# A two-layer graph network on one core: the f32 adjacency enters through 64 casting transfers issued by GpSimd and is recoded in place, instead of through strips cast by ScalarE and VectorE

## The chip, the core and the metric

The kernel runs on one core of a Trainium2 chip. A core has TensorE (PE, matrix products), VectorE (DVE), ScalarE (ACT), GpSimd (POOL) and SyncE (SP), which run side by side, each through its own list of instructions in order, and wait for one another at semaphores. Sixteen DMA engines move data between the device's memory and SBUF, the on-chip memory of 128 partitions. The metric is the time of one execution on the device in microseconds (us); lower is better.

## What is computed

x has 4096 nodes of 256 features, adj is a 4096 x 4096 matrix of zeros and ones in f32. The reference, cut to what matters:

```python
deg = jnp.maximum((adj != 0).astype(jnp.float32).sum(-1), 1.0)
x = _layernorm(x + _L0_gnn_ref(x, adj, deg[..., None], L0_gnn_W, L0_gnn_b), axis=-1)
x = _layernorm(x + _L1_gnn_ref(x, adj, adj, ...), axis=-1)

def _L0_gnn_ref(x, adjacency, node_degree, W, b):
    a_norm = dinv * (adjacency + eye) * dinv          # dinv = rsqrt(node_degree)
    return relu((a_norm @ x + x) @ W + b)

def _L1_gnn_ref(x, adj_a, adj_b, W_sa, a_sa, W_gcnb, b_gcnb, Wa, ba, Wb, bb):
    attn_a = sigmoid(concat([adj_a @ x, x], 1) @ Wa.T + ba)
    attn_b = sigmoid(concat([adj_b @ x, x], 1) @ Wb.T + bb)
    h = x @ W_sa
    scores = s_left[:, None] + s_right[None, :]       # both from h and a_sa
    e = where(adj_a != 0, exp(-leaky_relu(scores, 0.01)), 0.0)
    x_a = (e / (sum(e, axis=1) + 1e-05)) @ h
    x_b = adj_b @ (x @ W_gcnb) + b_gcnb
    return sigmoid(attn_a * x_a + attn_b * x_b)
```

## The kernel before

The 4096 rows are 32 tiles of 128 (`T`); the adjacency's columns are 16 panels of 256 (`PW`), two panels are a quad of four tiles, and there are 8 quads (`NQ`). The work has three stages.

**First products (0 to about 60 us).** x comes in six pieces (`x_in`, cut at tiles 0, 2, 4, 8, 16, 24, 32). A loop over the 32 tiles lets PE transpose a tile of x (L1333) and multiply it by W0 to z (L1348). ACT copies the transposed tile and, for the first 12 tiles, z; DVE copies z from tile 12 on (`ZACT`, L804). z is split into a high half (ACT, L529) and a low half (DVE, L831) in f16, after a scale that needs the largest value of x: DVE reduces each piece (L798), POOL reduces across partitions (L422). From step 14 on PE adds, in each step, one block of 128 adjacency rows to the sums of the first four tiles (`pass0_rows`, L1365). Between these, DVE and PE work out a norm of the weights; POOL raises it to a power (L425) for which DVE waits in `weight_scale` (L869 on) at step 25.

**First network (to about 323 us).** For each tile n PE sums 32 blocks of the adjacency, as fp8 codes, times z's halves (`sum_rows`, L1365; 64 matmuls). DVE makes degree, residual and statistics, POOL the reciprocal root (L441, a power) and the next tile's z plus bias (L434), DVE normalises (L990). PE transposes the result (`t_step`), ACT and DVE split it into two halves (L548, L946), PE projects it by the second network's weights (`p_step`, L1400). ACT copies the projections; POOL forms sums of them (`g_sums`, L278 to L280), ACT and DVE split those too (`forms_hi` L582 to L584, `forms_lo` L921 to L926).

**Second network (to the end).** 16 panels, each read back from a scratch in device memory into `pan` (L354 for the first two, L387 in the loop). DVE forms differences of panel blocks (L940), PE the products (L1470), ACT exponentials (L624), DVE masks them by the panel's codes (L1099), and PE multiplies them by h (L1529).

**How the adjacency comes in.** SP loads strips of 2 row blocks x 512 columns of f32 (512 KB, `strip`, a ring of 6; 128 strips, L341). Even strips are cast by ACT (L509), odd ones by DVE (L791), both to one byte per entry, 8 for an edge (2^-6 in fp8) and 128 (minus zero) for none, into `codes`, which holds three quads (`SLOTS`). A strip's slot in the ring comes free when it is cast, a quad's slot in `codes` when its four tiles are summed (`acc_done`) and its codes have been written to the scratch (`codes_out`, L329). SP issues the small weights after the fifth strip (`WTS_AT`). Where in its list an engine casts is written out by hand: `cast(count)` calls stand between its other steps.

## Time and profile before

| what | value |
|---|---|
| median of 3 runs | 880.51 us (879.71 to 880.66) |
| span of the profiled execution, first to last instruction | 877.3 us |
| busy: PE, DVE, ACT, POOL | 856.7, 683.4, 571.2, 181.3 us |
| granted TensorE clock, mean | 0.996 of full speed |
| DMA queue of SP / of ACT | 120.87 MB / 8.38 MB |

The profile is of one execution. For that execution only the span is given; the time of a whole run holds a few microseconds more than the span. Busy times of engines lie beside one another; a line such as L341 is a line of the kernel before.

### The profile page before, as it was taken

How to read it: one execution, taken by the hardware profiler on the slowest of the kernel's cores; microseconds unless marked ns; L12 is line 12 of the kernel's file. 1: busy time of each engine (PE TensorE's matmuls, PEld its weight loads, DVE VectorE, ACT ScalarE, POOL GpSimd, SP SyncE). 2: the span in 40 equal slices, each digit the busy share in tenths (PEclk: the TensorE clock that was granted, in tenths of full speed). 3: DMA queues.
4: the chain of work that ended last, by engine and by line, in shares of the span. 5: the costliest groups of instructions: out<-in, count | busy, mean ns of one | idle time of the engine just before them, and what ended most of it. 6: DMA issues, size and time to landing. Idle time of an engine off the chain costs nothing.

```text
span 877.3 us, 20460 instructions
## 1 busy us (share of the span) xinstructions
PE 856.7 (98%) x7579; PEld 755.0 (86%) x7579; DVE 683.4 (78%) x1182; ACT 571.2 (65%) x1214; POOL 181.3 (21%) x181
## 2 busy tenths in 40 slices
PE   8899999999999998999999999999999999999997
PEld 7787888888888887887788888888888888888886
DVE  5787676766667567898988988988978978978863
ACT  5754555555555237988977976966966967867831
POOL 1001333323322321012022022032032032032021
PEclk9999999999999999999999999999999999999999
DMA  9989999998999424110220120120120220220001
GB/s 321 305 273 320 352 401 339 360 344 315 380 316 341 174 105 144 56 55 1 79 80 15 63 78 24 54 78 15 63 78 6 71 78 0 78 78 0 25 25 37
DMA packets 66617, 130.01 MB, mean 148 GB/s; under 512 B 5464, under 2 KB 29056, under 8 KB 62080
## 3 DMA queue, kind: packets, MB, share of 16 engines
q1 hardware_dynamic: 57632, 120.87, 39.2%
q10 hardware_dynamic: 8928, 8.38, 2.8%
q8 instruction: 36, 0.59, 0.3%
q14 instruction: 21, 0.17, 0.1%
HBM read 99.87 MB, written 29.36 MB: 147 GB/s over the span
## 4 chain that ended last, share of the span: by engine, by line
PE 76%; issue 11%; DVE 5%; ACT 3%; DMA 3%; POOL 1%; SPq 0%; POOLq 0%; ACTq 0%; DVEq 0%
PE ps L1529 31%; PE ps L1365 21%; PE ps L1470 19%; PE ps L1400 4%; ACT ec L624 2%; DVE ec L1099 1%; DMA xs<-in_x_dram 1%; ACT em L633 1%; DMA h_scratch<-hst 1%; PE ps L1385 1%; DVE em L1106 1%; DVE dd L940 0%; POOL zb L434 0%; DMA x1r<-x_scratch 0%; SPq L335 0%
## 5 line engine op out<-in xcount | busy, mean ns | idle before, releaser
L1529 PE MATMUL ps<-fb,em 128*128 128x257 f16 x3072 | 347.5, 273 | 0.8 <-DVE em L1106 0.8
L1529 PEld LDWEIGHTS ps<-fb,em 128*128 128x128 f16 x3072 | 300.5, 98 | 38.6 <-issue 1.3
L1365 PE MATMUL ps<-y,codes 128*128 128x257 f16 x2048 | 237.8, 273 | 0.4 <-DVE y L831 0.4
L1365 PEld LDWEIGHTS ps<-y,codes 128*128 128x128 fp8e4 x2048 | 200.2, 98 | 27.0 <-DVE y L831 0.8
L624 ACT ACTIVATE ec<-slb,nsb 128x256 f32<-128x256 f32 x512 | 211.3, 499 | 0.0
L1106 DVE SCALAR_TENSOR_TENSOR em<-ec,em 128x2048 f16<-128x2048 f32 x64 | 147.4, 2303 | 22.7 <-ACT em L633 22.7
L633 ACT ACTIVATE em<-ec 128x2048 f16<-128x2048 f32 x64 | 122.1, 1910 | 65.1 <-PE ps L1529 57.0
L1099 DVE SCALAR_TENSOR_TENSOR ec<-ec,pan 128x2048 f32<-128x2048 f32 x64 | 147.3, 2302 | 2.6 <-issue 1.8
L1470 PE MATMUL ps<-zz,dd 128*128 128x256 f16 x768 | 89.4, 273 | 1.5 <-DVE t L1128 1.3
L458 POOL TENSOR_TENSOR sc<-sc,sc 128x2 f32<-128x2 f32 x15 | 38.5, 2569 | 246.3 <-DVE sc L1208 246.3
L1470 PEld LDWEIGHTS ps<-zz,dd 128*128 128x128 fp8e4 x768 | 75.0, 98 | 10.7 <-issue 2.0
L509 ACT ACTIVATE codes<-strip 128x1024 uint8<-128x1024 f32 x64 | 65.5, 1049 | 19.5 <-DMA strip<-in_adj_dram 18.6
L452 POOL TENSOR_TENSOR w<-w,bgb 128x512 f32<-128x512 f32 x16 | 27.7, 1732 | 184.6 <-DVE w L1166 184.6
L1470 PE MATMUL ps<-fa,pan 128*128 128x260 f16 x512 | 61.7, 279 | 3.4 <-DVE s L1137 2.1
L940 DVE SCALAR_TENSOR_TENSOR dd<-pan 128x512 uint32<-128x512 uint32 (+2 forms) x85 | 64.1, 815 | 0.0
L1470 PEld LDWEIGHTS ps<-fa,pan 128*128 128x128 fp8e4 x512 | 50.7, 99 | 11.6 <-issue 2.3
L441 POOL TENSOR_TENSOR lnst<-lnst,sc 128x1 f32<-128x1 f32 x32 | 24.8, 774 | 173.0 <-DVE lnst L984 173.0
L1470 PE MATMUL ps<-fa,dd 128*128 128x260 f16 x512 | 59.6, 274 | 0.4 <-DVE m L1118 0.4
L791 DVE TENSOR_SCALAR codes<-strip 128x1024 uint8<-128x1024 f32 x64 | 49.6, 777 | 10.7 <-DMA strip<-in_adj_dram 10.7
L1470 PEld LDWEIGHTS ps<-fa,dd 128*128 128x128 fp8e4 x512 | 49.9, 98 | 7.6 <-issue 0.9
L548 ACT ACTIVATE x1t<-ps 128x256 f16<-128x256 f32 x32 | 12.3, 383 | 60.0 <-PE ps L1385 60.0
L669 ACT ACTIVATE ot<-sg,sc 128x256 f32<-128x256 f32 x30 | 16.4, 593 | 52.5 <-POOL sc L462 52.5
(154 smaller groups left out, 786.0 us busy)
## 6 DMA issues: line engine op xcount, KB each, us to landing
strip<-in_adj_dram SPq DMA_DIRECT2D x128, 512.0 KB, 7.5
a_scratch<-codes SPq DMA_DIRECT2D x16, 1024.0 KB, 10.3
pan<-a_scratch SPq DMA_DIRECT2D x16, 1024.0 KB, 4.9
x_scratch<-x ACTq DMA_DIRECT2D x32, 128.0 KB, 5.3
x1r<-x_scratch SPq DMA_DIRECT2D x16, 256.0 KB, 2.8
h_scratch<-hst ACTq DMA_DIRECT2D x30, 136.0 KB, 5.5
out_dram<-ot SPq DMA_DIRECT2D x15, 256.0 KB, 2.2
fb<-h_scratch SPq DMA_DIRECT2D x3, 1088.0 KB, 8.8
```

Of the source, the lines that this page charges most:

```text
L458: pool.tensor_tensor(sc1[:, RS2], sc1[:, VE2], sc[:, MH2], ALU.pow).then_inc(S["yrstd_ready"], 1)
L509: act.activation(codes_of(s), strip_of(s), ACT.Copy, scale=float(EDGE - NONE), bias=float(NONE)).then_inc(S["cast_act"], 1)
L624: e_ = act.activation(ec[:, c % ER, jj, :], slb[:, slot, :], ACT.Exp, scale=-(1 - SLOPE), bias=nsb[:, jb:jb + 1])
L633: act.activation(em[:, c, 0], ec[:, c % ER], ACT.Copy, scale=MU / EDGE_VAL).then_inc(S["ehigh_ready"], 1)
L791: dve.tensor_scalar(codes_of(s), strip_of(s), float(EDGE - NONE), float(NONE), ALU.mult, ALU.add).then_inc(S["cast_dve"], 1)
L940: return dve.scalar_tensor_tensor(out=o, in0=b, scalar=0x7f7f7f7f, in1=a, op0=ALU.bitwise_and, op1=ALU.bitwise_xor)
L1099: dve.scalar_tensor_tensor(out=ec[:, c % ER], in0=ec[:, c % ER], scalar=1.0, in1=pan[:, slot, c * CH:(c + 1) * CH, :].bitcast(F8), op0=ALU ...
L1106: dve.scalar_tensor_tensor(out=em[:, c, 1], in0=ec[:, c % ER], scalar=MU / EDGE_VAL, in1=em[:, c, 0], op0=ALU.mult, op1=ALU.subtract).then ...
L1365: mm = pe.matmul(ACC(n), codes[:, qq % SLOTS, h, jb, e * P:(e + 1) * P].bitcast(F8), y[:, jb, part, 0:YC], start=(jb == 0 and part == 0), ...
L1400: mm = pe.matmul(b, x1t[:, n % 2, x_part, k * P:(k + 1) * P], wps[:, k, w_part, c0:c1], start=(k == 0 and x_part + w_part == 0), stop=(k = ...
L1470: mm = pe.matmul(ps[:, bank, 0:2 * c], a.bitcast(F8), g, start=(p == 0), stop=(p == NP - 1))
L1529: mm = pe.matmul(PH(2 * m + e)[:, 0:HC], em[:, c, e_part, i, e * P:(e + 1) * P], fb[:, jb, h_part, 0:HC], start=(jb == 0 and e_part + h_pa ...
```

## The change

The strips, their ring and all casts go. POOL issues 64 transfers (`load_codes`), each of 4 row blocks x 512 columns: 1 MB of f32 is read, and the DMA engines write it as fp8 straight into a quad's slot of `codes`. There an edge is 0x38 and no edge 0x00; DVE recodes a chunk in place over 32-bit words (`code`): an exclusive or with 0x20 in each byte, then a shift left by two bits, which gives 0x60 (32.0) and 0x80 (minus zero). The constant `EDGE_VAL` goes from 2^-6 to 32 in all scales. DVE recodes at the places where it cast; ACT's casts at their places are gone. Each of the 24 chunks that fit into `codes` has its own semaphore. `codes` and the scratch now keep a quad's 512 columns of a row block together, so the quad's codes leave in one transfer of 2 MB, and a panel is read back as 256 bytes per row block and partition. SP loads the small weights right after x. PE, SP and ACT wait for DVE's recodes alone (`coded`). The first chunks are issued when the fifth piece of x has come (`x_in[4]`).

```diff
-SJ = 2
-GS = T // SJ
-NSTRIP = NQ * GS
-RING = 6
+CJ = 4
+GS = T // CJ
+NCHUNK = NQ * GS
...
-EDGE, NONE = 8, 128
-EDGE_VAL = 2.0 ** -6
+EDGE_VAL = 32.0
+ZERO_BIT, RAISE = 0x20202020, 2
...
-    codes = at("codes", [P, SLOTS, 2, T, PW], U8, O_C)
-    strip = at("strip", [P, RING, SJ, 2 * PW], F32, O_S)
+    codes = at("codes", [P, SLOTS, T, 2 * PW], U8, O_C)
...
-    a8d = nc.dram_tensor("a8_scratch", [NPAN, P, T, PW], U8)
+    a8d = nc.dram_tensor("a8_scratch", [NQ, P, T, 2 * PW], U8)
...
-            def codes_when_cast(qq):
-
-                for sem, n in zip(("cast_act", "cast_dve"), casts_until(qq * GS + GS - 1)):
-                    sp.wait_ge(S[sem], n)
-                for h in range(2):
-                    sp.dma_start(a8d[2 * qq + h], codes[:, qq % SLOTS, h]).then_inc(codes_out[qq % SLOTS], 16)
+            def codes_when_coded(qq):
+
+                sp.wait_ge(S["coded"], (qq + 1) * GS)
+                sp.dma_start(a8d[qq], codes[:, qq % SLOTS]).then_inc(codes_out[qq % SLOTS], 16)
...
-            for s in range(NSTRIP):
-                if s >= RING:
-                    sp.wait_ge(S["cast_act" if on_act(s - RING) else "cast_dve"],
-                               casts_until(s - RING)[0 if on_act(s - RING) else 1])
-                qq, g = s // GS, s % GS
-                sp.dma_start(strip[:, s % RING], adj_view[:, g * SJ:(g + 1) * SJ, qq * 2 * PW:(qq + 1) * 2 * PW]
-                             ).then_inc(strip_in[s % RING], 16)
-                if s == WTS_AT:
-                    load_weights()
-                if s >= RING and (s - RING) % GS == GS - 1:
-                    codes_when_cast((s - RING) // GS)
+            load_weights()
+            for qq in range(NQ - 1):
+                codes_when_coded(qq)
...
-                sp.dma_start(pan[:, m], a8d[m]).then_inc(panel_in[m], 16)
+                sp.dma_start(pan[:, m], a8d[0, :, :, m * PW:(m + 1) * PW]).then_inc(panel_in[m], 16)
...
-                sp.dma_start(pan[:, m], a8d[s + 2]).then_inc(panel_in[m], 16)
+                sp.dma_start(pan[:, m], a8d[bass.ds(qq, 1), :, :, m * PW:(m + 1) * PW].rearrange("q p t i -> p (q t) i")
+                             ).then_inc(panel_in[m], 16)
...
+            def load_codes(c0, c1):
+
+                for c in range(c0, c1):
+                    qq, g = c // GS, c % GS
+                    if qq >= SLOTS and g == 0:
+                        pool.wait_ge(S["acc_done"], PT * (qq - SLOTS + 1))
+                        pool.wait_ge(codes_out[qq % SLOTS], 16 * (qq // SLOTS))
+                    pool.dma_start(codes[:, qq % SLOTS, g * CJ:(g + 1) * CJ, :].bitcast(F8),
+                                   adj_view[:, g * CJ:(g + 1) * CJ, qq * 2 * PW:(qq + 1) * 2 * PW]
+                                   ).then_inc(codes_in[c % (SLOTS * GS)], 16)
+
             pool.wait_ge(S["const_ready"], 2)
             pool.wait_ge(S["wabs_ready"], 1)
             pool.partition_all_reduce(wabs[:, 1, :], wabs[:, 0, :], P, RADD).then_inc(S["wz_all"], 1)
+            pool.wait_ge(x_in[4], 16)
+            load_codes(0, 3)
             pool.wait_ge(S["xmax_part"], 1)
             pool.partition_all_reduce(sc[:, XALL], sc[:, XMX], P, RMAX).then_inc(S["xmax_all"], 1)
 
+            load_codes(3, SLOTS * GS)
             pool.wait_ge(S["wnorm_ready"], 1)
             pool.tensor_tensor(sc[:, WN], sc[:, WMX], sc[:, MH], ALU.pow).then_inc(S["alpha_pow"], 1)
...
                 if n + 2 < T:
                     z_with_bias(n + 2)
+                first = SLOTS * GS + (n - PT + 1) * 2
+                if SLOTS * GS <= first < NCHUNK:
+                    load_codes(first, first + 2)
                 if n == 3:
                     g_sums(pool, 0)
                 if n >= 4 and n % 2 == 0:
...
-        def cast_waits(eng, s):
-
-            qq = s // GS
-            eng.wait_ge(strip_in[s % RING], 16 * (s // RING + 1))
-            if qq >= SLOTS:
-                eng.wait_ge(S["acc_done"], PT * (qq - SLOTS + 1))
-                eng.wait_ge(codes_out[qq % SLOTS], 32 * (qq // SLOTS))
...
-            def cast(count):
-
-                for s in [next(todo) for _ in range(count)]:
-                    cast_waits(act, s)
-                    act.activation(codes_of(s), strip_of(s), ACT.Copy, scale=float(EDGE - NONE),
-                                   bias=float(NONE)).then_inc(S["cast_act"], 1)
-
...
-            for sem, n in zip(("cast_act", "cast_dve"), casts_until(NSTRIP - 1)):
-                act.wait_ge(S[sem], n)
+            act.wait_ge(S["coded"], NCHUNK)
...
-            def cast(count):
-
-                for s in [next(todo) for _ in range(count)]:
-                    cast_waits(dve, s)
-                    dve.tensor_scalar(codes_of(s), strip_of(s), float(EDGE - NONE), float(NONE),
-                                      ALU.mult, ALU.add).then_inc(S["cast_dve"], 1)
+            def code(count):
+
+                for c in [next(todo) for _ in range(count)]:
+                    dve.wait_ge(codes_in[c % (SLOTS * GS)], 16 * (c // (SLOTS * GS) + 1))
+                    words = codes[:, c // GS % SLOTS, c % GS * CJ:(c % GS + 1) * CJ, :].bitcast(U32)
+                    dve.tensor_scalar(words, words, ZERO_BIT, RAISE, ALU.bitwise_xor, ALU.logical_shift_left
+                                      ).then_inc(S["coded"], 1)
 
...
                 if t % 2 == 0:
-                    cast(1)
+                    code(1)
...
 
-            def rows_cast(qq, jb):
-
-                strip_nr = qq * GS + jb // SJ
-                mine = 0 if on_act(strip_nr) else 1
-                pe.wait_ge(S[("cast_act", "cast_dve")[mine]], casts_until(strip_nr)[mine])
+            def rows_coded(qq, jb):
+
+                pe.wait_ge(S["coded"], qq * GS + jb // CJ + 1)
...
-                        mm = pe.matmul(ACC(n), codes[:, qq % SLOTS, h, jb, e * P:(e + 1) * P].bitcast(F8),
+                        mm = pe.matmul(ACC(n), codes[:, qq % SLOTS, jb, (2 * h + e) * P:(2 * h + e + 1) * P].bitcast(F8),
```

On POOL, at its start: what stands there before, from the sum of the weights' absolute values (`wabs`, L420) to the first reciprocal root. L422 is the maximum across partitions, L425 the power, L434 z plus bias.

```order
L420 ISA wabs<-wabs 128x256 [waits wabs_ready,const_ready]
L422 ISA sc<-sc 128x1 [waits xmax_part]
L425 ISA
L425 TENSOR_TENSOR sc<-sc 128x1 [waits wnorm_ready]
L434 TENSOR_TENSOR zb<-zf,b0b 128x256 [waits zf_act,wts_in]
L434 TENSOR_TENSOR zb<-zf,b0b 128x256 [waits zf_act]
```

And the same place of the changed kernel (its L414, L418, L422 and L431 are L420, L422, L425 and L434 of before):

```order
L414 ISA wabs<-wabs 128x256 [waits wabs_ready,const_ready]
L408 DMA codes<-in_adj_dram 128x4x512 [waits x_in4]
L408 DMA codes<-in_adj_dram 128x4x512 x2
L418 ISA sc<-sc 128x1 [waits xmax_part]
L408 DMA codes<-in_adj_dram 128x4x512 x21
L422 ISA
L422 TENSOR_TENSOR sc<-sc 128x1 [waits wnorm_ready]
L431 TENSOR_TENSOR zb<-zf,b0b 128x256 [waits zf_act,wts_in]
```

Three transfers now stand ahead of the maximum across partitions, and twenty-one ahead of the power.

On POOL, at tile 3 of the first network: before, from that tile's reciprocal root (L441) to the next tile's.

```order
L441 TENSOR_TENSOR lnst<-lnst,sc 128x1 [waits stat_ready]
L434 TENSOR_TENSOR zb<-zf,b0b 128x256 [waits zf_act,r_ready]
L278 TENSOR_TENSOR gb<-gb 128x258 [waits g_ready]
L279 TENSOR_TENSOR fs<-gb 128x128
L280 TENSOR_TENSOR fs<-gb 128x256
```

And of the changed kernel (L438, L431 and L269 to L271 are L441, L434 and L278 to L280 of before):

```order
L438 TENSOR_TENSOR lnst<-lnst,sc 128x1 [waits stat_ready]
L431 TENSOR_TENSOR zb<-zf,b0b 128x256 [waits zf_act,r_ready]
L408 DMA codes<-in_adj_dram 128x4x512 [waits codes_out0,acc_done]
L408 DMA codes<-in_adj_dram 128x4x512
L269 TENSOR_TENSOR gb<-gb 128x258 [waits g_ready]
L270 TENSOR_TENSOR fs<-gb 128x128
L271 TENSOR_TENSOR fs<-gb 128x256
```

Two transfers stand between POOL's addition and its three sums; the same pair follows the addition at each tile up to tile 22.

On DVE, at step 12 of the first loop: before, the copy of z, the first two low halves and a cast.

```order
L804 COPY zf<-ps 128x256 [waits z_done,sx_ready]
L831 SCALAR_TENSOR_TENSOR y<-zf,sc,y 128x256 [waits yhi_ready] x2
L791 TENSOR_SCALAR codes<-strip 128x2x2x256 [waits strip_in1]
L804 COPY zf<-ps 128x256 [waits z_done]
L831 SCALAR_TENSOR_TENSOR y<-zf,sc,y 128x256 [waits yhi_ready]
```

And of the changed kernel (L768, L795 and L755 are L804, L831 and L791 of before):

```order
L768 COPY zf<-ps 128x256 [waits z_done,sx_ready]
L795 SCALAR_TENSOR_TENSOR y<-zf,sc,y 128x256 [waits yhi_ready] x2
L755 TENSOR_SCALAR codes<-codes 128x512 [waits codes_in0]
L768 COPY zf<-ps 128x256 [waits z_done]
L795 SCALAR_TENSOR_TENSOR y<-zf,sc,y 128x256 [waits yhi_ready]
```

The recode has the cast's place. It is of chunk 0, the first four row blocks; the cast was of strip 1, row blocks 2 and 3, with strip 0 on ACT.

## Rows read from the trace of the kernel before

**Rows 1.** The page's first part: busy us, share of the span, instructions.

```profile
PE 856.7 (98%) x7579; PEld 755.0 (86%) x7579; DVE 683.4 (78%) x1182; ACT 571.2 (65%) x1214; POOL 181.3 (21%) x181
```

**Rows 2.** Table by stretch: length, busy us of each engine, clock, DMA share, GB/s.

```profile
20.00:50.00 30.00, 26.95 (x182) 21.96 (x180) 21.10 (x56) 20.52 (x44) 2.04 (x4) 1.00 0.93 307
50.00:91.00 41.00, 39.05 (x324) 33.44 (x323) 31.30 (x85) 19.04 (x41) 6.30 (x11) 1.00 0.88 298
100.00:323.00 223.00, 222.68 (x2021) 197.63 (x2019) 148.82 (x402) 108.05 (x268) 66.15 (x93) 1.00 0.86 309
```

**Rows 3.** The chain that ended last, two pieces: start us, us, what.

```profile
308.02 3.52 PE ps L1365 x32
...
316.61 3.52 PE ps L1365 x32
```

**Rows 4.** Groups of instructions; then one row of the timeline near 335 us.

```profile
L509 ACT ACTIVATE codes<-strip 128x1024 uint8<-128x1024 f32 x64 | 65.5, 1049 | 19.5 <-DMA strip<-in_adj_dram 18.6
L791 DVE TENSOR_SCALAR codes<-strip 128x1024 uint8<-128x1024 f32 x64 | 49.6, 777 | 10.7 <-DMA strip<-in_adj_dram 10.7
...
335.08 0.49 DVE L1063 TENSOR_SCALAR slb<-slb,sc 128x512 f32<-128x512 f32 x1
```

**Rows 5.** Timeline, 14 to 30 us: start, us, instruction [idle before <-releaser].

```profile
14.20 2.29 DVE L798 TENSOR_REDUCE sc<-xs 128x1 f32<-128x2048 f32 x1 [0.59 <-DMA xs<-in_x_dram]
...
17.07 2.29 DVE L798 TENSOR_REDUCE sc<-xs 128x1 f32<-128x2048 f32 x1 [0.59 <-DMA xs<-in_x_dram]
...
19.65 0.39 POOL L422 PARTITION_ALL_REDUCE sc<-sc  x1 [8.75 <-DVE sc L894]
...
22.44 0.87 DVE L831 SCALAR_TENSOR_TENSOR y<-zf,sc,y 128x256 f16<-128x256 f32 x2
...
23.16 1.04 PE L1365 MATMUL ps<-y,codes 128*128 128x257 f16 x8
...
29.00 0.22 PE L1421 MATMUL ps<-ident,wrow 8*128 8x8 f32 x1 [1.75 <-DMA sc<-in_L_gnn_bb_dram]
```

**Rows 6.** Timeline, 45 to 57 us, around the power and what follows it.

```profile
46.16 0.60 POOL L425 TENSOR_TENSOR sc<-sc 128x1 f32<-128x1 f32 x1 [26.12 <-DVE sc L864]
...
52.02 0.15 DVE L869 TENSOR_SCALAR sc<-sc 128x1 f32<-128x1 f32 x1
...
53.25 0.42 DVE L804 COPY zf<-ps 128x256 f32<-128x256 f32 x1 [0.17 <-PE ps L1348]
...
56.11 1.03 PE L1348 MATMUL ps<-w,xt 128*128 128x256 f32 x4
```

**Rows 7.** Timeline, 88 to 97 us, around tile 3's sums on POOL.

```profile
88.43 0.55 POOL L441 TENSOR_TENSOR lnst<-lnst,sc 128x1 f32<-128x1 f32 x1 [4.28 <-DVE lnst L984]
...
90.69 0.63 POOL L280 TENSOR_TENSOR fs<-gb 128x256 f32<-128x256 f32 x1
...
91.36 0.42 ACT L582 ACTIVATE fa<-gb 128x260 f16<-128x260 f32 x1 [2.77 <-POOL fs L280]
...
92.53 0.43 DVE L921 TENSOR_TENSOR fa<-gb,fa 128x260 f16<-128x260 f32 x1 [2.71 <-ACT zz L584]
...
95.92 1.50 PE L1400 MATMUL ps<-wps,x1t 128*128 128x262 f16 x12 [0.93 <-DVE x1t L946]
```

**Rows 8.** DMA queues of SP (q1) and ACT (q10): packets, MB, share.

```profile
q1 hardware_dynamic: 57632, 120.87, 39.2%
q10 hardware_dynamic: 8928, 8.38, 2.8%
```

**Rows 9.** Timeline of the second network: a panel's issue, its first use.

```profile
482.17 0.35 SPq L387 DMA_DIRECT2D pan<-a_scratch  x1
...
519.56 4.17 DVE L940 SCALAR_TENSOR_TENSOR dd<-pan 128x512 uint32<-128x512 uint32 x5
```

**Rows 10.** One line's instructions: DVE's normalisation; duration ns min/median/max.

```profile
L990 DVE TENSOR_SCALAR x<-x,lnst x32: 399/805/830, 74.9 to 327.7; 128x256 f32<-128x256 f32 x32
```

**Rows 11.** Groups: POOL's addition; busy us, mean ns.

```profile
L434 POOL TENSOR_TENSOR zb<-zf,b0b 128x256 f32<-128x256 f32 x32 | 27.0, 844 | 0.0
```

More of the change, by code:

```diff
@@ L129, in build @@
     ec = at("ec", [P, ER, CH, PW], F32, O_S)
-    area = Area(O_S + RING * SJ * 2 * PW * 4, O_L1)
+    area = Area(O_S + 3 * CH * PW * 4, O_L1)
     x1 = area("x1", [P, X1RING, D], F32)
@@ L261, in build @@
         adj_view = adj.rearrange("(j p) c -> p j c", p=P)
-        on_act = lambda s: s % 2 == 0
-        def casts_until(s):
-            mine = sum(on_act(i) for i in range(s + 1))
-            return mine, s + 1 - mine
         def z_is_copied(eng, t):
@@ L351, in _ @@
             for slot in (0, last):
-                sp.wait_ge(codes_out[slot], 32 * len(range(slot, NQ - 2, SLOTS)))
+                sp.wait_ge(codes_out[slot], 16 * len(range(slot, NQ - 2, SLOTS)))
             for m in range(2):
-                sp.dma_start(pan[:, m], a8d[m]).then_inc(panel_in[m], 16)
+                sp.dma_start(pan[:, m], a8d[0, :, :, m * PW:(m + 1) * PW]).then_inc(panel_in[m], 16)
             sp.wait_ge(S["ex_ready"], PT)
@@ L495, in split_at @@
             return range(upto(t - 1), T if t == T else upto(t))
-        ACT_CASTS = [s for s in range(NSTRIP) if on_act(s)]
-        DVE_CASTS = [s for s in range(NSTRIP) if not on_act(s)]
         @block.scalar
         def _(act):
-            todo = iter(ACT_CASTS)
-            def cast(count):
-                for s in [next(todo) for _ in range(count)]:
-                    cast_waits(act, s)
-                    act.activation(codes_of(s), strip_of(s), ACT.Copy, scale=float(EDGE - NONE),
-                                   bias=float(NONE)).then_inc(S["cast_act"], 1)
             def xt_copy(t):
@@ L536, in _ @@
                     y_hi(i)
-                if t >= 11 and t % 2 == 1:
-                    cast(1)
             for t in split_at(T):
@@ L585, in forms_hi @@
                                ).then_inc(S["ghi_ready"], 1)
-            cast(3)
             x1t_copy(0)
-            cast(1)
             proj_copies(0)
             x1t_copy(1)
-            cast(1)
             proj_copies(1)
@@ L596, in _ @@
             forms_hi(0)
-            cast(1)
             proj_copies(2)
@@ L600, in _ @@
             proj_copies(3)
-            cast(3)
             for n in range(PT + 2, T + 3):
@@ L604, in _ @@
                     proj_copies(n - 3)
-                more = n // PT + 1 < NQ and n < T
                 if n - 2 < T:
@@ L609, in _ @@
                     forms_hi((n - 3) // 2)
-                if more:
-                    cast(2)
-            assert next(todo, None) is None
             def exp_chunk(s, slot, c, nth=0, first=False, behind={}):
@@ L731, in _ @@
             for j in range(SLOTS):
-                act.wait_ge(codes_out[j], 32 * len(range(j, NQ, SLOTS)))
+                act.wait_ge(codes_out[j], 16 * len(range(j, NQ, SLOTS)))
             high_chunk(0, 0, True)
@@ L779, in _ @@
             st = Steps(dve, S["dve_step"])
-            todo = iter(DVE_CASTS)
+            todo = iter(range(NCHUNK))
             dve.memset(sc[:, MH], -0.5)
@@ L904, in _ @@
                 if t % 2 == 0:
-                    cast(1)
+                    code(1)
                 if WT_AT <= t < WT_AT + 4:
@@ L915, in _ @@
                 y_lo(t)
-            cast(3)
+            code(3)
             def forms_lo(p):
@@ L1002, in _ @@
             normalize(1)
-            cast(1)
+            code(1)
             head(2)
@@ L1007, in _ @@
             x1t_lo(1)
-            cast(2)
+            code(2)
             head(3)
@@ L1013, in _ @@
             forms_lo(0)
-            cast(1)
+            code(1)
             h_lo(2)
             x1t_lo(3)
-            cast(1)
+            code(1)
             head(4)
@@ L1020, in _ @@
             normalize(4)
-            cast(2)
+            code(2)
             for n in range(PT + 2, T + 3):
@@ L1042, in _ @@
                 if more:
-                    cast(1)
+                    code(1)
                 if n - 1 < T:
@@ L1046, in _ @@
                 if more:
-                    cast(1)
+                    code(1)
                 if T - 2 <= n <= T:
@@ L1361, in sum_rows @@
                 for jb in range(j0, j1):
-                    if jb % SJ == 0 and n % PT == 0:
-                        rows_cast(qq, jb)
+                    if jb % CJ == 0 and n % PT == 0:
+                        rows_coded(qq, jb)
                     for part in range(2):
-                        mm = pe.matmul(ACC(n), codes[:, qq % SLOTS, h, jb, e * P:(e + 1) * P].bitcast(F8),
+                        mm = pe.matmul(ACC(n), codes[:, qq % SLOTS, jb, (2 * h + e) * P:(2 * h + e + 1) * P].bitcast(F8),
                                        y[:, jb, part, 0:YC], start=(jb == 0 and part == 0),
```

21 lines of the change are left out of this document (9 added, 12 removed).

## The prediction

> **What bounds the kernel now.** I read the busy times first, then a table by stretch, then the chain, then the stretches in which PE waits.
>
> TensorE (PE) works 856.7 of 877.3 us [rows 1]: whatever the change frees elsewhere, it can give back at most the part of PE's 20.6 us of idleness that handling the adjacency causes. By stretch [rows 2], PE idles 3.05 us of the 30 from 20 to 50 us, 1.95 us of the 41 up to 91, and 0.32 us of the 223 from 100 to 323. So the long stretch, in which most of the adjacency is loaded and the first network's sums run, is PE's alone: a group of 32 matmuls at 308.02 has its counterpart at 316.61, one tile in 8.59 us [rows 3]. There VectorE (DVE) is busy 148.82 of 223 us, 5.73 per tile, ScalarE (ACT) 108 and GpSimd (POOL) 66.
>
> The casts cost 65.5 us on ACT and 49.6 on DVE [rows 4], nearly all beside PE's work. They matter only where PE stands: near 20 to 30 us and near 75 to 98 us. At the start [rows 5] the scale is late: the sixth piece of x is in at 17.07, the maximum across partitions runs on POOL at 19.65, the first low halves at 22.44, PE's first sums at 23.16; at 29.00 PE has stood 1.75 us for the last of the small weights, issued behind the first strips. Near 88 to 96 us [rows 7] PE hangs on a relay: POOL's power (88.43), POOL's three sums (the last at 90.69), ACT's copy at 91.36 after 2.77 us of waiting, DVE at 92.53 after 2.71, PE at 95.92 after 0.93.
>
> **The change, part by part.** The profile gives the span alone, 877.3; the median of the runs, 880.51, lies 3.21 above it, and I carry that 3.21 over.
>
> *The issue on POOL* is the unknown price, g for one transfer of 512 rows; POOL issues no DMA now. From below: SP issues a 1 MB transfer in 0.35 us [rows 9]. From above: if POOL takes one step per row, 512 steps at the pace of its addition over 256 elements, 0.844 us [rows 11], are 1.69 us. Neither is nearer in kind, so I take the middle, 1.02. Only a page has a price: the Trainium skill, DMA: Bandwidth & Descriptors, section Latency and other measured facts, gives about 1 us to the first byte for a transfer that GpSimd issues; with 1.0 the sum below is the same.
>
> *Three issues before the maximum.* They start when the fifth piece is in (14.20, the maximum over it) and must end by 19.65: 5.45 us, so up to g = 1.8 POOL's idle time there hides them. *Twenty-one more* run from about 20.04 to 41.5 us. POOL's next task now starts at 46.16 after 26.12 us of idling for DVE [rows 6], so they fit up to g = 1.24. Beyond that DVE, which picks the power up at 52.02 (5.86 later), waits and holds back its copies of z behind it; PE needs the copy of 53.25 + 0.42 for its product at 56.11, 2.4 us of slack. So PE loses from 26.1 + 5.9 + 2.4 = 34.4 us of issuing on, g = 1.64; the upper bound costs 21 x 1.69 - 34.4 = 1.1 us.
>
> *A pair of issues ahead of the sums at tile 3.* They stand between POOL's addition and the three sums of rows 7, for which ACT waits: 2g = 2.0 us on the relay. ACT's cast (1.05 us) between those copies and the next projection's goes, and DVE's recode is shorter by 0.3; I put the relay's end 0.6 earlier than a plain shift, between those two. **+1.4** (2 x 0.35 - 0.6 = +0.1 to 2 x 1.69 - 0.6 = +2.8). In later tiles the pairs fall into POOL's idle time: 66 us of work and 40 x 1.02 are 107 of 223.
>
> *The recode on DVE.* Nearest row: a tensor-scalar in place over 512 32-bit words, 0.49 us [rows 4]; upper bound the cast's mean, 0.78. It frees 64 x 0.29 = 18 us of DVE, hidden behind PE except between 75 and 97 us, where DVE leads PE and some five recodes lie in its line; PE's waits there are under 1 us apiece and have other causes too, so **-0.5** (0 to -0.9). Against that, the first rows now come from DVE alone: ACT had cast its strip long before, DVE recodes after its first two low halves (22.44 + 0.87 = 23.31) and ends at 23.8, where PE had begun at 23.16 with its weights fetched just before: **+0.8**.
>
> *The front of the queue.* The weights follow x directly, so the wait at 29.00 shrinks, but the first transfers share the DMA engines with them: **-1.0** (0 to -1.75). The sixth piece of x may share them with the first transfer: **+0.5** (0 to +2.87, the spacing of the two maxima in rows 5, if its rate halves).
>
> *The transfers* read the same 67 MB of f32. Before, 57,632 packets took 39.2% of 16 engines [rows 8], 95 ns each; 32 per engine make 3.06 us for 1 MB; at the long stretch's 309 GB/s it is 3.4. PE's last quad of tiles begins near 323 - 4 x 8.59 = 288.6; from 16 us on, 64 transfers may take 4.26 us each before PE waits. Below, if only the written quarter counted, 0.8 us, which gains nothing where PE is full. I take 3.1 to 3.4: 0; the five tiles between a pair's issue and its recode hide the latency.
>
> *The panels.* In the scratch a panel's row is now 32 pieces of 256 B, not 8 KB: 4096 pieces, 256 per engine. At the 44 ns of the 8,928 packets in ACT's 2.8% [rows 8] that is 11.3 us, at 95 ns 24.4, and not less than if nothing changed. A panel issued at 482.17 is first used by DVE at 519.56 [rows 9], 37 us later: 0. Only the first two panels, with the row vectors queued behind them, could slip: 0 to +3.
>
> Sum: 1.4 - 0.5 + 0.8 - 1.0 + 0.5 = **+1.2 us**: a span of 878.5, a time of **881.7 us**. All low bounds: 0.1 - 0.9 + 0.8 - 1.75 = -1.75 (878.8); all high ones: 1.1 + 2.8 + 0.8 + 2.87 + 3 = +10.6 (891.1).
>
> **The rivals.** *Slow issue.* g above 1.69: nothing in the trace excludes it, each transfer having 512 rows with two addresses. It decides from g = 1.64 on, where DVE waits for the power (52.02 now). g = 2.0: 42 - 34.4 = 7.6, before the maximum 3 x 2.0 - 5.45 = 0.6, at tile 3 3.4, the rest -0.2: about 892. g = 2.5: 18.1 + 2.1 + 4.4 - 0.2, about 905.
>
> *Slow casting transfers.* If converting halves the rate to 6.8 us, PE ends 64 x (6.8 - 4.26) = 163 us later, about 1044. It decides from 4.26 us on. Against it: the read side is unchanged, and a quarter is written.
>
> *A shared port.* DVE's normalisation has a median of 805 ns and a minimum of 399 [rows 10]; in most tiles it starts with POOL's addition (0.844 us) at its side. So recode and issue may hold each other up. One issue per recode adds 2.0 us to DVE's 5.73 per tile, which PE's 8.59 hides; both issues per recode add 4.1, and 5.73 + 4.1 - 0.57 saved is 0.7 over, in some 22 tiles 15 us. I price it at +2 to +15 beside the main sum, middle 890. The Trainium skill, SBUF — State Buffer, section Who interferes with whom, has it as a rule: a tensor-scalar in a two-port mode and a GpSimd instruction shut each other out, and descriptors that GpSimd writes starve meanwhile. By that rule the sum would be this rival's; 399 against 805 agrees with it, but no run here shows an issue beside such an instruction.
>
> *Faster.* ACT without its casts copies x earlier, and PE's other idleness up to 91 us (5.0 less the 1.75 for the weights) halves: -1.75 - 1.6 + 0.1, some 3 us, 877.3. Against it: ACT is busy only 20.5 of the 30 us from 20 to 50, so it is not what PE mostly waits for. More than PE's idleness can't come.
>
> **How the numbers follow.** Main case 0.58, likeliest 881.7, own range 878.8 to 891; slow issue 0.14; slow transfers 0.09; port 0.09; faster 0.10. 0.2%, 1.76 us, is about what a measurement of this kernel can tell from no change. Of the main case I put 0.34 within it and 0.24 above 882.27. So faster 0.10, same 0.34, slower 0.24 + 0.14 + 0.09 + 0.09 = 0.56: the likeliest single case is a loss inside the limit, but what may go wrong lies nearly all on one side. The range 877.8 to 894 holds the main case, most of the port's and part of the slow issue's; the slow transfers and the ends, about 0.2, are out.
>
> **What would show it.** POOL's 21 issues end before 46 us and its power still waits for DVE; if not, the issue was mis-sized. The wait at 29.00 is under 1 us. ACT's copy after the first sums waits about 2 us longer than 2.77. The recode takes 0.4 to 0.5 us; well over that, the port speaks. PE idles under 1 us from 100 to 323. Panels land within 25 us and nobody waits for them. The prediction is wrong if PE waits for recoded rows after 60 us, if DVE stands at the power, or if the second half changes at all.

## The result and the profile after

The changed kernel takes 875.24 us (median of 4 runs, 874.96 to 876.12) against 880.59 (4 runs, 879.71 to 881.17) of the kernel before: ratio 0.9934, 95% interval 0.9919 to 0.9949. A second set of runs gives 875.83 against 880.44, ratio 0.9948 (0.9932 to 0.9964). I had predicted 881.7 in a range from 877.8 and had called a gain the least likely outcome. It is a gain of 0.5 to 0.7%.

The first part of the page of the changed kernel stands against [rows 1]: the other engines moved much (ACT 571 to 509, POOL 181 to 225), PE only from 856.7 to 855.1.

```profile
span 874.3 us, 20237 instructions
PE 855.1 (98%) x7579; PEld 755.0 (86%) x7579; DVE 667.5 (76%) x1182; ACT 508.7 (58%) x1150; POOL 225.3 (26%) x245
q0 software_dynamic: 33792, 16.78, 23.7%
```

The front of the changed kernel (the first products, up to about 60 us), for [rows 5]. The columns are start, duration, instruction, and the idle time before it with its releaser:

```profile
17.21 2.29 DVE L762 TENSOR_REDUCE sc<-xs 128x1 f32<-128x2048 f32 x1 [0.63 <-DMA xs<-in_x_dram]
24.42 0.43 DVE L755 TENSOR_SCALAR codes<-codes 128x512 uint32<-128x512 uint32 x1 [2.03 <-DMA codes<-in_adj_dram]
24.99 1.04 PE L1327 MATMUL ps<-y,codes 128*128 128x257 f16 x8 [1.68 <-DVE codes L755]
29.01 0.22 PE L1383 MATMUL ps<-ident,wrow 8*128 8x8 f32 x1
```

The weights are no longer waited for. But DVE now stands 2.03 us for the first transfer and PE starts its sums at 24.99 instead of 23.16. At 29.0 both kernels are level.

Next, the stretch from 61 to 94 us, first of the kernel before (rows that the prediction did not show), then of the changed one:

```profile
61.41 14.25 PE L1365 MATMUL ps<-y,codes 128*128 128x257 f16 x128 [0.36 <-DVE y L831]
68.24 0.69 DVE L791 TENSOR_SCALAR codes<-strip 128x1024 uint8<-128x1024 f32 x1 [2.55 <-DMA strip<-in_adj_dram]
71.03 0.69 DVE L791 TENSOR_SCALAR codes<-strip 128x1024 uint8<-128x1024 f32 x1 [2.10 <-DMA strip<-in_adj_dram]
71.64 0.15 DVE L956 TENSOR_SCALAR lnst<-ps 128x1 f32<-128x1 f32 x1
75.78 0.44 PE L1385 MATMUL ps<-ident,x 128*128 128x128 f32 x2
78.63 1.50 PE L1400 MATMUL ps<-wps,x1t 128*128 128x262 f16 x12 [0.66 <-DVE x1t L946]
84.69 1.50 PE L1400 MATMUL ps<-wps,x1t 128*128 128x262 f16 x12 [0.82 <-DVE x1t L946]
89.77 1.49 PE L1400 MATMUL ps<-wps,x1t 128*128 128x262 f16 x12
```

```profile
60.91 14.25 PE L1327 MATMUL ps<-y,codes 128*128 128x257 f16 x128 [0.36 <-DVE y L795]
67.28 0.16 DVE L920 TENSOR_SCALAR lnst<-ps 128x1 f32<-128x1 f32 x1 [1.96 <-PE ps L1327]
75.00 0.38 PE L1347 MATMUL ps<-ident,x 128*128 128x128 f32 x2
85.79 1.71 POOL L408 DMA_DIRECT2D codes<-in_adj_dram  x2
87.11 1.49 PE L1362 MATMUL ps<-wps,x1t 128*128 128x262 f16 x12
89.19 0.42 ACT L555 ACTIVATE fa<-gb 128x260 f16<-128x260 f32 x1 [3.26 <-POOL fs L271]
93.75 1.50 PE L1362 MATMUL ps<-wps,x1t 128*128 128x262 f16 x12 [1.41 <-DVE x1t L910]
```

Before, DVE stood twice for strips just ahead of its work on tile 0 (L956), which began at 71.64. After, the same work (L920) waits for PE and begins at 67.28. The stretch from PE's first transposition to its third projection takes 89.77 - 75.78 = 13.99 us before and 87.11 - 75.00 = 12.11 after. Counted from the start of PE's block of 128 products of the first sums (61.41 and 60.91), the third projection comes after 28.36 and 26.20 us: 2.16 us, of which 0.28 lie ahead of the transposition. The fourth projection then comes later, because of the pair of issues at 85.79: 6.15 us behind the third before [rows 7], 6.64 after.

By this yardstick the 3.0 us between the two spans (877.3, 874.3) are: 0 at 29.0; -0.78 from there to the first transposition (75.78 to 75.00), 0.51 of it ahead of PE's block of 128 products; -1.88 to the third projection; +0.49 to the fourth; -0.70 to the fifth (105.21 to 102.34); -0.1 behind it. From the end of the first sums (322.9 and 319.9) both take 554.4 us to the end, so the second network did not change.

In the table by stretch PE no longer idles at all from 100 us to the end of the first sums, against the third row of [rows 2] (the row from 46 to 60 us is for experiment 11):

```profile
46.00:60.00 14.00, 14.00 (x97) 12.03 (x96) 9.64 (x30) 7.32 (x19) 1.67 (x3) 1.00 1.23 153
100.00:320.00 220.00, 220.00 (x2001) 195.89 (x2000) 135.05 (x394) 61.90 (x220) 87.81 (x128) 1.00 0.89 147
```

### The profile page after: what moved, and what is told of

Its sections match the earlier page's. It is cut to its first block, busy times and chain, and to the rows that moved or that the text cites. A ratio compares the mean times of both kernels' runs of the same rounds, so it can differ in the third digit from the quotient of the medians.

```text
span 874.3 us, 20237 instructions
## 1 busy us (share of the span) xinstructions
PE 855.1 (98%) x7579; PEld 755.0 (86%) x7579; DVE 667.5 (76%) x1182; ACT 508.7 (58%) x1150; POOL 225.3 (26%) x245
## 3 DMA queue, kind: packets, MB, share of 16 engines
q0 software_dynamic: 33792, 16.78, 23.7%
## 4 chain that ended last, share of the span: by engine, by line
PE 77%; issue 8%; DVE 5%; ACT 4%; POOL 3%; DMA 2%; SPq 0%; POOLq 0%; ACTq 0%; DVEq 0%
PE ps L1491 31%; PE ps L1327 21%; PE ps L1432 19%; PE ps L1362 4%; POOL codes L408 2%; ACT ec L588 2%; DMA xs<-in_x_dram 1%; DVE ec L1063 1%; ACT em L597 1%; PE ps L1347 1%; DVE em L1070 1%; DVE dd L904 0%; POOL zb L431 0%; DMA x1r<-x_scratch 0%; DVE sc L762 0%
## 5 line engine op out<-in xcount | busy, mean ns | idle before, releaser
L536 ACT ACTIVATE q<-ps,sc 128x1 f32<-128x1 f32 x32 | 11.2, 351 | 108.8 <-PE ps L1362 108.8
L438 POOL TENSOR_TENSOR lnst<-lnst,sc 128x1 f32<-128x1 f32 x32 | 21.7, 677 | 155.6 <-DVE lnst L948 155.6
L920 DVE TENSOR_SCALAR lnst<-ps 128x1 f32<-128x1 f32 x32 | 5.0, 156 | 66.7 <-PE ps L1327 66.7
L408 POOL DMA_DIRECT2D codes<-in_adj_dram x64 | 49.7, 795 | 2.7 <-DMA xs<-in_x_dram 2.7
```

Source lines behind the costliest of these rows:

```text
L408: pool.dma_start(codes[:, qq % SLOTS, g * CJ:(g + 1) * CJ, :].bitcast(F8), adj_view[:, g * CJ:(g + 1) * CJ, qq * 2 * PW:(qq + 1) * 2 * PW] ...
```

## The experiments

Two theories for the gain. **Late input:** VectorE no longer stands for strips ahead of tile 0. **Engine time:** the relay is shorter because ScalarE has no casts and VectorE's recode is shorter than its cast.

**1. The reorder alone (b_head_early).** In the kernel before, the third of three casts goes behind tile 0's normalisation:

```diff
-            cast(3)
+            cast(2)
...
             normalize(0)
+            cast(1)
             head(1)
```

> The kernel before, with one of the three VectorE casts that stand ahead of its work on tile 0 moved behind that tile's normalisation (the strip it needs came only at 71.03). Theory 1, late input: the gain of the change came from VectorE no longer standing there for strips (2.55 and 2.10 us). Then the work on tile 0 starts near 68.9 instead of 71.64, TensorE's first projection near 76.5 to 77.5 instead of 78.63, and the span falls by 1.0 to 2.0 us, to 875.3 to 876.3. Theory 2, engine time: the gain came from ScalarE without its casts (1.05 us each) and VectorE's shorter recode. Then this reorder, which leaves all casts in place, gives under 0.4 us: 876.9 to 877.4.

Median 879.24 (12 runs) against 881.33 (23 runs), ratio 0.9976 (0.9966 to 0.9986). Its profile, PE alone:

```profile
30.64 0.27 PE L1422 MATMUL ps<-ident,wrow 8*128 8x8 f32 x1 [3.48 <-DMA sc<-in_L_gnn_bb_dram]
78.57 0.38 PE L1386 MATMUL ps<-ident,x 128*128 128x128 f32 x2
90.68 1.49 PE L1401 MATMUL ps<-wps,x1t 128*128 128x262 f16 x12
```

From 78.57 to 90.68 are 12.11 us: the whole 1.88 of the changed kernel, with every f32 strip and every cast in place. The absolute times that I expected (tile 0 at 68.9, a span of 875.3 to 876.3) were missed: the wait for the weights was 3.48 us in this profile instead of 1.75, everything behind it stands later, and the span is 878.0. The wait had a second price: behind it PE's granted clock is 0.50 from 31 to 33 us, the lower of its two levels (1.2 GHz), where it is 1.00 in the kernel before.

```profile
31.00:33.00 2.00, 2.00 (x11) 1.58 (x10) 0.17 (x2) 0.00 (x0) 0.00 (x0) 0.50 1.05 402
```

So PE's last products of the first stage stand 3.07 us later than before (62.23 for 59.16): 1.64 come up to the weights, 1.43 behind them. VectorE's tile 0 stands only 0.2 later (71.82 for 71.64). A later front alone does not do that: the next experiment's kernel and two more profiles of the kernel before have fronts 0.6 to 3.5 us later, tile 0 later by 0.6 to 3.8, and a stretch of 13.98 to 13.99 us. From the start of PE's block to the third projection they take 28.38 to 28.58 us, the reordered kernel 26.20.

**2. The weights' place alone (b_weights_first).** `WTS_AT = 0` instead of 4.

> The kernel before, with the small weights issued behind the first strip instead of the fifth. Theory 1, the wait at 29.00 is worth its whole 1.75 us wherever nothing else takes its place: TensorE's first sums stay at 23.16, the wait is gone, the span falls by 1.0 to 1.75 us, to 875.5 to 876.3. Rival: the four strips behind the weights come about 2.5 us later and VectorE or ScalarE stand for them, so that most of it is given back: 876.7 to 877.4.

Median 882.68 against 881.33, ratio 1.0021 (1.0010 to 1.0032): slower. The wait at the weights is gone and another, longer one has come before it, for a product whose input ACT copies late, since ACT stood for a strip:

```profile
26.43 1.06 ACT L509 ACTIVATE codes<-strip 128x1024 uint8<-128x1024 f32 x1 [4.33 <-DMA strip<-in_adj_dram]
27.80 1.40 PE L1348 MATMUL ps<-w,xt 128*128 128x256 f32 x4 [3.82 <-ACT xt L517]
```

So here the reorder moved the wait from the weights to a strip, and made it longer; the granted clock is 0.50 from 30 to 31 us, behind that wait, and tile 0 begins at 75.40. In the changed kernel, too, a wait stands in place of the one at the weights, 1.68 us at the first transfer. Experiment 6 shows that it can be removed there without another in its place.

**3 and 4. ScalarE's time (a_act_busy), VectorE's time (a_dve_long).** Work of the old length is put back into the changed kernel.

```diff
+                    act.activation(dumb[:, i % 8], dum[:], ACT.Copy, scale=-120.0, bias=128.0).then_inc(S["dummy"], 1)
```

> The changed kernel, with 64 copies of 1024 elements from f32 to bytes put back on ScalarE at the places of the old casts, on a tile of constants that nobody else reads (about 1.05 us each; the output is not touched). Theory 1, late input: ScalarE's time was not what the relay hung on, span within 0.5 us of 874.3. Theory 2, engine time: the relay of 70 to 100 us gets its old length back, 1.2 to 2.5 us more, 875.5 to 876.8.

```diff
+                    dve.tensor_scalar(dumb[:, c % 8], dum[:], ZERO_BIT, RAISE, ALU.bitwise_xor,
+                                      ALU.logical_shift_left).then_inc(S["dummy"], 1)
```

> The changed kernel, with one more VectorE operation over 256 words behind each of the 64 recodes (about 0.27 us, which makes the pair as long as an old cast; its result is not used). Theory 1, late input: within 0.4 us of 874.3. Theory 2, engine time: 0.5 to 0.9 us more, since some five recodes stand in VectorE's line between 75 and 97 us.

Medians 876.35 (ratio 0.9944, 0.9931 to 0.9957) and 876.57 (0.9948, 0.9935 to 0.9961), spans 874.5 and 875.2. The intervals overlap those of the changed kernel; the profiles say more. Third and fourth projection of a_act_busy, then third to fifth of a_dve_long:

```profile
87.34 1.49 PE L1385 MATMUL ps<-wps,x1t 128*128 128x262 f16 x12
93.98 1.50 PE L1385 MATMUL ps<-wps,x1t 128*128 128x262 f16 x12 [1.41 <-DVE x1t L933]
```

```profile
87.01 1.49 PE L1368 MATMUL ps<-wps,x1t 128*128 128x262 f16 x12
94.17 1.50 PE L1368 MATMUL ps<-wps,x1t 128*128 128x262 f16 x12 [1.93 <-DVE x1t L916]
103.18 1.50 PE L1368 MATMUL ps<-wps,x1t 128*128 128x262 f16 x12 [0.25 <-DVE x1t L916]
```

With ScalarE as busy as before, every distance is that of the changed kernel to 0.01 us; all rows stand 0.23 later, as its first sums do. ScalarE's casts were free. With VectorE's old length the fourth projection comes 7.16 us behind the third instead of 6.64, and the fifth 9.01 behind the fourth instead of 8.59. That is 0.52 + 0.42 = 0.94 us that the shorter recode is worth there. It is worth another 0.26 us in the front: from the product behind the weights to PE's block of 128 products the longer recode takes 32.16 us (28.65 to 60.81), the changed kernel 31.90 (29.01 to 60.91). Together these are 1.20 us, and none of it lies between the first transposition and the third projection, which are 12.11 us apart in both.

**5. The pair of issues (a_sums_first).** In the changed kernel, POOL's three sums go ahead of its issues in each tile:

```diff
-                first = SLOTS * GS + (n - PT + 1) * 2
-                if SLOTS * GS <= first < NCHUNK:
-                    load_codes(first, first + 2)
                 if n == 3:
                     g_sums(pool, 0)
                 if n >= 4 and n % 2 == 0:
                     g_sums(pool, (n - 2) // 2)
+                first = SLOTS * GS + (n - PT + 1) * 2
+                if SLOTS * GS <= first < NCHUNK:
+                    load_codes(first, first + 2)
```

> The changed kernel, with GpSimd's three sums ahead of the pair of issues in every tile that has both. In the changed kernel the sums at tile 3 stood behind the pair and TensorE waited 1.41 us at its fourth projection (93.75). Theory, the pair costs what the relay shows: the sums start 1.7 us earlier, the wait falls to 0.4 us or less, and the fourth projection comes 0.8 to 1.2 us sooner after the third than the 6.64 us of before this edit; span 873.2 to 873.5. My prediction had 1.4 us for the pair: 872.9. Rival, something else (the recodes, ScalarE's copies) sets that wait: 874.0 to 874.5.

```profile
86.76 1.49 PE L1362 MATMUL ps<-wps,x1t 128*128 128x262 f16 x12
92.28 1.50 PE L1362 MATMUL ps<-wps,x1t 128*128 128x262 f16 x12 [0.29 <-DVE x1t L910]
```

Median 874.18, ratio 0.9934 (0.9913 to 0.9954), span 872.8. Third to fourth projection 5.52 us instead of 6.64: the pair cost 1.12 us there. The ratio is that of the changed kernel's first set and does not tell the two apart; the rows do. Of the 1.5 us between the two spans 0.35 is an earlier start of the first sums (24.64 for 24.99).

**6 and 7. The first transfer in halves (a_first_half), and both edits (a_half_sums).** The first transfer becomes two of two row blocks, each recoded by itself:

```diff
+                if c0 == 0:
+                    for i, sem in enumerate((half_in, codes_in[0])):
+                        pool.dma_start(codes[:, 0, 2 * i:2 * i + 2, :].bitcast(F8),
+                                       adj_view[:, 2 * i:2 * i + 2, 0:2 * PW]).then_inc(sem, 16)
```

> The changed kernel, with the first transfer split into two of two row blocks each, each half recoded by itself. In the changed kernel VectorE stood 2.03 us for the first transfer (24.42) and TensorE 1.68. Theory, that lateness takes back what the weights' earlier place gives: the first sums start 1.2 to 1.8 us earlier, at 23.2 to 23.8, the small weights are still in time, and the span falls by 1.0 to 1.8 us, to 872.5 to 873.3. Rival, the front is bound by what the DMA engines deliver as a whole, so the wait only moves to the next half or to the weights: under 0.5 us, 873.8 to 874.3.

> The two edits to the changed kernel together (first transfer in two halves, GpSimd's sums ahead of the issues). They stand 65 us apart and meet in nothing, so the gains should add: 871.3 to 872.7 if both theories hold, 873.8 to 874.5 if neither does.

```profile
22.55 1.04 PE L1341 MATMUL ps<-y,codes 128*128 128x257 f16 x8
26.57 0.22 PE L1397 MATMUL ps<-ident,wrow 8*128 8x8 f32 x1
```

```profile
23.01 1.04 PE L1341 MATMUL ps<-y,codes 128*128 128x257 f16 x8
85.42 1.49 PE L1376 MATMUL ps<-wps,x1t 128*128 128x262 f16 x12
90.49 1.49 PE L1376 MATMUL ps<-wps,x1t 128*128 128x262 f16 x12
```

a_first_half: 874.86, ratio 0.9940 (0.9926 to 0.9955), span 872.5, the sums 2.4 us sooner and nothing in place of the wait. So the rival, a front bound by the DMA engines as a whole, fell for this kernel. The median is only 0.4 to 1.0 us below the two of the changed kernel, the profiled span 1.8. Both together: **873.51**, ratio **0.9920** (0.9906 to 0.9935), span 871.6, the fastest kernel of this study by the median, though its interval still overlaps those of the changed kernel. Here PE waits neither at the first sums nor at its first four projections.

**8 and 9. The kernel before, again (before_again, before_third).**

> The kernel before, unchanged, for a second look at the wait for the small weights. In its first profile that wait was 1.75 us and the span 877.3; in the profile of the reordered kernel, whose first 60 us are the same, it was 3.48 and the start of the second stage 1.6 us later. Theory, the wait differs from run to run and the profile that I predicted from had a short one: here 1.5 to 3.5 us, and the span larger by as much as the wait is. Rival, the difference was the reorder's: 1.7 to 1.8 again, span 877 to 877.5.

> The kernel before once more, for the wait for the small weights (1.75 and 2.01 us in its two profiles, 3.48 in the reordered kernel's): between 1.7 and 3.5, and the start of tile 0's work on VectorE at 71.5 to 73.5, late by about what the wait adds.

Waits for the weights of 2.01 and 2.26 us, tile 0 at 72.28 and 72.61, spans of 877.7 and 877.9, times of the profiled runs 879.88 and 880.0: 2.1 to 2.2 us above the span. Their medians, 880.49 and 881.48, lie 0.6 and 1.5 above the profiled runs.

**10. The changed kernel, again (after_again).**

> The changed kernel again, for its scatter. Four runs of it had spans of 873.2 to 874.3, and the profiled one was the longest. If the old kernel's scatter of 3 us comes from the weights that wait behind strips, this one, which has no such wait, stays within 1.5 us: 874.5 to 876.5, spans 873 to 874.5. If it is the chip's, it scatters by 3 us as well.

Six runs from 874.61 to 877.26, median 875.83; the profiled run 876.68 at a span of 874.9, so 1.8 above its span. It scatters by 2.65 us, the old one in its two sets by 3.0 and 4.6. Neither statement held cleanly.

**11 and 12. How deep the queue is (a_ring, b_ring4).** In the changed kernel a transfer waits until the one three before it is recoded; in the kernel before the ring has four strips instead of six.

```diff
+                    if c >= 3:
+                        pool.wait_ge(S["coded"], c - 2)
```

> The changed kernel, in which GpSimd issues a transfer only when the one three before it is recoded, so that 3 MB of f32 at most are under way or waiting, as in the old ring of six strips. GpSimd's sums stand ahead of its issues here, since they must. Theory 1a, the changed kernel's rows are early because 24 transfers are queued ahead of their use: now the DMA engines run less from 46 to 60 us, VectorE stands again for the rows ahead of tile 0, its work there starts after 69 instead of 67.3, and the span is 1 to 4 us above the changed kernel with the same order of sums (872.8): 873.8 to 877. Theory 1b, they are early because a casting transfer writes a quarter of the bytes and so comes sooner, whatever the depth: 872.5 to 873.3, tile 0 near 67.

```diff
-RING = 6
+RING = 4
...
-WTS_AT = 4
+WTS_AT = 3
```

> The kernel before with four strips in its ring instead of six, the small weights issued one strip earlier so that they stand behind no wait; SP issues the strips and waits for nothing else, so nothing but the strips is held up. Theory 1a, the depth of what is queued ahead of the casts sets when rows arrive: from 46 to 60 us the queue moves clearly less than the 3.4 MB of the kernel before, VectorE starts on tile 0 later than 71.6 to 72.6, and the span grows by 1.5 us or more, beyond 879. Theory 1b, the rate of the transfers alone sets it, whatever the depth: arrivals as before, tile 0 at 71.5 to 72.6, span 876.5 to 878.

892.66 (ratio 1.0139, 1.0118 to 1.0160) and 888.43 (1.0092, 1.0072 to 1.0112): far slower, both in the direction of depth, and a_ring well beyond the figures that I gave. In a_ring the DMA engines fall to a busy share of 0.37 from 46 to 60 us (1.23 in the changed kernel; packets of its two queues overlap, so the share can pass 1) and VectorE stands 12.2 us for its rows. But POOL's power stood behind the waits as well, and VectorE waited 4.2 us for it, so the size says little:

```profile
46.00:60.00 14.00, 12.37 (x88) 10.40 (x87) 7.71 (x27) 5.91 (x16) 3.66 (x5) 1.00 0.37 22
DVE codes L758 <- DMA codes<-in_adj_dram: 12.2, 5, 5.1
```

In b_ring4 SP waits, as before, only for the casts. It loses from 30 to 46 us, at 252 GB/s against 300, not from 46 to 60 as I had written, and tile 0 begins at 74.94. The write of the codes also stands two strips earlier in its list (issued at 54.97), but the loss comes ahead of that.

**13. The write of the codes (b_write_later).** In the kernel before, the two transfers of each quad's codes to the scratch, 2 MB, go into SP's queue eight strips later.

```diff
-                if s >= RING and (s - RING) % GS == GS - 1:
-                    codes_when_cast((s - RING) // GS)
+                if s >= RING + GS and (s - RING) % GS == 7:
+                    codes_when_cast((s - RING) // GS - 1)
```

> The kernel before, with each quad's two transfers of codes to the scratch (2 MB) issued eight strips later. In the kernel before the first of them stand at 55.57 in SP's queue, ahead of the strips that VectorE and ScalarE then waited for (66.98 to 72.39). Theory W, it is this write that makes those strips late: they come 3 to 5 us sooner, VectorE's waits of 2.55 and 2.10 us and TensorE's waits at its first two projections go, tile 0 starts near 68 to 69, and the span falls by 1.5 to 2.5 us, to 875.0 to 876.4 at a wait of 1.75 us for the weights. Theory D, it is the depth of the ring alone: tile 0 at 71 to 72.6, first to third projection's stretch as before (13.98 us from the first transposition to the third projection), span 877 to 878. Both may hold in part.

The issue that is moved, in the kernel before, and then what stands ahead of tile 0 in the new kernel:

```profile
55.57 1.92 SPq L329 DMA_DIRECT2D a_scratch<-codes  x2
57.54 16.30 SPq L341 DMA_DIRECT2D strip<-in_adj_dram  x11
```

```profile
69.63 0.69 DVE L791 TENSOR_SCALAR codes<-strip 128x1024 uint8<-128x1024 f32 x1 [0.61 <-DMA strip<-in_adj_dram]
70.52 0.16 DVE L956 TENSOR_SCALAR lnst<-ps 128x1 f32<-128x1 f32 x1 [0.20 <-PE ps L1365]
78.24 0.38 PE L1385 MATMUL ps<-ident,x 128*128 128x128 f32 x2
90.34 1.49 PE L1400 MATMUL ps<-wps,x1t 128*128 128x262 f16 x12
124.97 1.50 PE L1400 MATMUL ps<-wps,x1t 128*128 128x262 f16 x12 [2.59 <-DVE x1t L946]
```

Ahead of tile 0 VectorE's waits for strips are down to 0.61 us, tile 0 waits for PE, and the stretch takes 12.10 us. So the write ahead of those strips was enough to make them late. The kernel as a whole gains nothing by it: 882.66 against 881.37, ratio 1.0015 (1.0001 to 1.0029). In this profile the wait for the weights was 2.61 us, the granted clock is 0.50 from 32 to 34 us behind it, and PE's block of 128 products starts at 64.15 instead of 61.41. And a wait of 2.59 us stands at 124.97 that the kernel before has not: VectorE stood 6.05 us for a strip up to 121.60, after the next quad's write had gone into the queue at 103.68. That the stand moved along with the write is likely; no run tests it.

## Why the prediction was wrong

**The step that failed** is the term for the transfers: "I take 3.1 to 3.4: 0". I compared the transfers' rate with what PE uses and found room, which held: PE never waited for rows after 60 us. But I did not ask where in the queues a strip stands. In the kernel before, strips and the codes' write share SP's queue, and a strip is issued only when a cast has freed its place. In the changed kernel 24 transfers are queued by 36 us on POOL's queue and the write has SP's to itself. The two queues' totals up to 55 us, first of before, then of after:

```profile
q1 hardware_dynamic: 11610, 16.31, 89.1%
q0 software_dynamic: 7180, 3.57, 78.5%
q1 hardware_dynamic: 6016, 5.51, 32.7%
```

The changed kernel's 5.51 MB on q1 are x and the weights; less these, before has 10.8 MB of strips in. After has 4 x 3.57 = 14.3, since q0 counts the written quarter. Where I took 3.1 to 3.4 us for a transfer, the first thirteen land 2.54 us apart (24.40 to 54.91). Before, strips that were queued also came fast, 1.37 us for half as much (18.39 to 23.85), but the next one landed only at 30.26; it had been issued at 21.48, behind the weights.

What came of the late strips was in the trace that I had: the 2.55 and 2.10 us ahead of tile 0. I read PE's waits in that stretch as "under 1 us apiece", and did not follow the two at the projections back to VectorE's stand at 71.03. Shown: the reorder alone and the write's move alone each give the 1.88 us of that stretch, and 2.2 us from PE's block on. In the time of the whole kernel only the reorder shows it (2.1 us between the medians); the moved write brings other waits. Shown too: a shallower ring makes input later. What depth alone would give without the write was not taken apart.

**Point by point.**
- *Issue:* 0.79 us (mean 795 ns of 64), taken as 1.02. The 21 fit; POOL's power still waited 10.0 us for DVE. The slow issue fell.
- *The pair at tile 3:* +1.4, measured 1.12. As the relay arrived early, ACT's wait grew only from 2.77 to 3.26, not by 2.
- *Recode:* 0.42 us (0.49), its worth 1.20 us (0.5, bound 0.9). I looked for it from 75 us on only; 0.26 of it lie in the front.
- *First rows:* +0.8, measured +1.83. I counted DVE's order and not when the first transfer lands: it is issued at 14.59 and lands at 24.40. From 14 to 24 us SP's queue still moved 1.64 MB of x and the weights; that this held it up is not shown.
- *Weights:* -1.0. The whole 1.75 went, and the line above took it back. The two are not one limit: with half as large a first transfer (experiment 6) both waits are gone.
- *Sixth piece of x:* +0.5, measured 0.14 (17.07 to 17.21).
- *Panels:* landing 7.0 us after issue at the median (4.9 before), hidden as predicted.
- *What lies around the span:* I carried 3.21 us over. In all runs whose span is known it is 2.0 to 2.2 before and 1.7 to 1.8 after. So the first profile was of a run about 1 us below the median of its set, and this went into the 3.21. Of the 6.5 us by which the time was missed, 4.2 are the span (878.5 for 874.3) and 2.3 this: the changed kernel's median lies 0.94 above its profiled span, not 3.21.
- *The sum:* the terms that I had, as measured, cancel (+1.83 and -1.75 in the front, +1.12 and -1.20 for the pair and the recode) instead of adding 1.2. Late input is -2.2. Some 0.7 of the 3.0 us are in small waits that no experiment singles out.
- *Slow transfers* fell with PE's full stretch from 100 us. *Faster* named ACT's casts as the cause; a_act_busy refutes that. That its 877.3 was the nearest of all forecasts is luck.
- *The port* fell as a price: DVE has room for it. Its place is seen, though. The recode at 118.91, beside POOL's addition, takes 0.95 us, the one at 110.71, beside an issue, 0.41, as most of the 64 do (median 0.42):

```profile
118.59 0.99 POOL L431 TENSOR_TENSOR zb<-zf,b0b 128x256 f32<-128x256 f32 x1
118.91 0.95 DVE L755 TENSOR_SCALAR codes<-codes 128x512 uint32<-128x512 uint32 x1
...
110.59 1.59 POOL L408 DMA_DIRECT2D codes<-in_adj_dram  x2
110.71 0.41 DVE L755 TENSOR_SCALAR codes<-codes 128x512 uint32<-128x512 uint32 x1
```

The Trainium skill, SBUF — State Buffer, section Who interferes with whom, has a tensor-scalar in a two-port mode and a GpSimd instruction shut each other out. The first pair agrees with it; the second shows no such hold-up, neither of the recode nor of the two issues (1.59 us, at a mean of 0.795 for one).

None of the signs that I had listed as making the prediction wrong came up. The list had only new waits on it, and no wait of the old kernel that might go.

**Left open.** The medians differ by 4.6 to 5.4 us, the profiled spans by 3.0, and 0.3 to 0.4 of the rest lie around the span. The span is known of 101 runs of the kernel before, with a median of 879.0, and of ten of the changed one, with a median of 873.8. So the first profile, 877.3, shows a short run of the kernel before, and some 2 us of the gain lie in runs without a trace. The front is a candidate, not a proof. The wait for the weights was 1.75, 2.01, 2.26, 2.61 and 3.48 us in five profiles with the old front, and there is none after. Behind the two longest of these PE's clock fell, and the way from the weights to PE's block took 1.4 to 1.7 us more (33.84 and 34.09 us for 32.41).

## What to carry to other kernels

Before pricing an edit to a data stream, list the waits of the old kernel for that stream, and follow each to the bound engine, however small the waits are there: a queue in which loads stand behind a write, or behind buffers that free late, can cost more than the work on the data. An engine's freed time is worth only what stands in line on a relay; here one engine's 65 us were worth nothing and another's shorter operation 1.2. Take the profiled run's own time for what lies around the span, not the median.
